# Twenty-four extra transposes inside a recurrence, twelve on float32 cells and twelve on float32r cells

## The reference

```
z = sigmoid(x @ Wz + bz);  h_tilde = x @ Wh + bh
a, b = 1 - z, z * h_tilde
h[s] = a[s] * h[s-1] + b[s]          (a scan along the sequence)
x = layernorm(x + sigmoid(h @ Wg + bg) * h)
```

## Time and profile before

| | |
|---|---|
| median of three runs | 854.05 us |
| the profiled execution, whole time | 854.72 us |
| its span, first to last instruction | 852.9 us |
| busy share of the span: TensorE / VectorE / ScalarE / GpSimd | 94 / 77 / 71 / 50 % |
| TensorE busy from 33 to 45.4 us (two steps of the recurrence) | 12.40 of 12.40 us |
| mean granted TensorE clock | 0.996 |

### The profile page before, as it was taken

One profiled execution on the slowest core, in us unless ns is written; L12 is line 12 of the kernel. 1 busy time (PEld: TensorE's weight loads), 2 busy tenths in 40 slices (PEclk: granted clock), 3 DMA queues, 4 the chain that ended last, 5 costly groups with the idle time before them and its releaser, 6 DMA issues.

```text
span 852.9 us, 20803 instructions
## 1 busy us (share of the span) xinstructions
PE 805.5 (94%) x6837; PEld 605.5 (71%) x6837; DVE 654.1 (77%) x2466; ACT 609.7 (71%) x1595; POOL 427.7 (50%) x459
## 2 busy tenths in 40 slices
PE   9998999999999988999999999999999999999996
PEld 8876776766667766677777767667766777677785
DVE  4987778888998766777777667673888888985667
ACT  4547887888784367877877777774899999985341
POOL 2255667666644155254552534224665666425763
PEclk9999999999999999999999999999999999999999
DMA  9401761112103368977868688756122211100001
GB/s 321 157 25 45 224 194 51 55 60 81 70 15 124 124 216 269 295 218 242 277 205 268 215 247 255 239 177 212 42 66 67 66 66 66 64 2 1 26 25 50
DMA packets 105392, 115.64 MB, mean 136 GB/s; under 512 B 28589, under 2 KB 93869, under 8 KB 105030
## 3 DMA queue, kind: packets, MB, share of 16 engines
q1 hardware_dynamic: 104724, 113.97, 41.8%
q10 hardware_dynamic: 562, 0.35, 0.1%
HBM read 48.70 MB, written 51.82 MB: 118 GB/s over the span
## 4 chain that ended last, share of the span: by engine, by line
PE 46%; ACT 9%; DVE 5%; issue 3%; DMA 2%; POOL 1%; SPq 0%; DVEq 0%; ACTq 0%; POOLq 0%
PE bank L1544 7%; PE bank L242 6%; PE bank L250 4%; PE bank L2259 4%; PE bank L1559 3%; PE bank L2245 3%; ACT bias_area L2597 2%; PE bank L2276 2%; PE bank L1528 2%; PE bank L1585 2%; PE bank L1595 2%; PE bank L2309 2%; PE bank L2353 2%; PE bank L2347 2%; ACT Sx L1750 2%
## 5 line engine op out<-in xcount | busy, mean ns | idle before, releaser
L242 PE MATMUL bank<-x_feat,w_all_mats 128*128 128x256 f32 x384 | 92.7, 386 | 1.8 <-ACT q_full L358 0.6
L2994 POOL TENSOR_TENSOR bnd<-bnd,consts 128x60 f32<-128x60 f32 x64 | 18.1, 305 | 142.0 <-DMA bnd<-band_scratch 142.0
L242 PEld LDWEIGHTS bank<-x_feat,w_all_mats 128*128 128x128 f32 x384 | 70.5, 191 | 14.3 <-ACT rw L2639 3.8
L2597 ACT ACTIVATE bias_area<-bias_area,mq_two 128x256 f32<-128x256 f32 x128 | 66.2, 529 | 0.0
L1003 DVE COPY q_heads<-bank 128x512 f32<-128x512 f32 x64 | 42.0, 684 | 24.4 <-PE bank L717 24.4
L2773 DVE COPY q_heads<-bank 128x512 f32<-128x512 f32 x64 | 41.2, 683 | 23.2 <-PE bank L2259 23.2
L896 ACT ACTIVATE Sx<-Sx,mq 128x256 f32<-128x256 f32 x128 | 54.4, 498 | 5.4 <-DVE mq L995 5.4
L1750 ACT ACTIVATE Sx<-Sx,mq 128x256 f32<-128x256 f32 x128 | 54.3, 500 | 3.4 <-DVE mq L1848 3.4
L904 ACT ACTIVATE q_heads<-bank 128x512 f32<-128x512 f32 x64 | 37.8, 590 | 26.3 <-PE bank L717 26.3
L1856 DVE COPY q_heads<-bank 128x512 f32<-128x512 f32 x64 | 42.0, 684 | 17.0 <-PE bank L1544 17.0
L896 ACT ACTIVATE Pr<-Pr,mq 128x256 f32<-128x256 f32 x128 | 54.4, 502 | 0.9 <-DVE mq L995 0.9
(11 more groups left out here) (309 smaller groups left out, 2384.8 us busy)
## 6 DMA issues: line engine op xcount, KB each, us to landing
dist<-skew_scratch SPq DMA_DIRECT2D x64, 296.0 KB, 4.1
skew_scratch<-rw SPq DMA_DIRECT2D x30, 588.0 KB, 4.5
bnd<-band_scratch SPq DMA_DIRECT2D x64, 108.0 KB, 2.6
band_scratch<-bias_area SPq DMA_DIRECT2D x32, 162.0 KB, 2.5
band_scratch<-bias_area SPq DMA_DIRECT2D x32, 148.0 KB, 2.1
skew_scratch<-dist SPq DMA_DIRECT2D x4, 1024.0 KB, 7.1
context_values<-dist SPq DMA_DIRECT2D x8, 512.0 KB, 2.6
v_two<-context_values SPq DMA_DIRECT2D x8, 512.0 KB, 4.3
```

The source lines that it names most:

```text
L242: last = pe.matmul(dst[:, m * S:(m + 1) * S], w[:, k, m * P:(m + 1) * P], rhs[:, k, :], start=(k == 0), stop=(k == FT - 1))
L2597: last = act.activation(rows_of(n, g)[:, t, :], rows_of(n, g)[:, t, :], ACT.Exp, bias=mq_two[:, n % 2, g, t:t + 1], scale=-1.0, accum_out= ...
```

## The change

- SyncE: at the end of `first_loads` it waits for the small tables and all thirteen matrices, and then issues two copies of 64 KB within SBUF: the identity `ident` and one 128x128 block of `sa_Wq`, into two float32r tensors within the space of `q_par` (which the attention fills later).
- TensorE: after `gate_product(4)` it waits for these copies, and turns the block of `sa_Wq` twelve times from float32 into bank 3 and twelve times from the float32r copy into bank 5. All twelve of a kind have the same input; four places of a bank are written three times each.
- VectorE: after its loop, with `norm` of batch 5 begun, it waits for the last transpose, copies 16 columns of bank 3 to SBUF, subtracts them from 16 columns of bank 5, and adds the result times 1e30 to the 16 ones of `v_two` for one tile of tokens. Each of the three waits for the one before.

```diff
+        raw_ident = exact_cells("raw_ident", [P, P], q_par_at)
+        raw_x = exact_cells("raw_x", [P, P], q_par_at + 4 * P)
+        raw_in, raw_mm, raw_steps = sem("raw_in"), sem("raw_mm"), sem("raw_steps")
+        raw_rows = sb("raw_rows", [P, 2, H])
+        def raw_loads(sp):
+            sp.wait_ge(loaded_small, 48)
+            sp.wait_ge(loaded_w, 16 * len(WMATS[3:]))
+            sp.dma_start(raw_ident[:, :].bitcast(F32), ident[:, :]).then_inc(raw_in, 16)
+            sp.dma_start(raw_x[:, :].bitcast(F32), W["sa_Wq"][:, 0, 0:P]).then_inc(raw_in, 16)
+        def raw_turns(pe):
+            pe.wait_ge(raw_in, 32)
+            for i in range(12):
+                pe.transpose(bank[3][:, i % 4 * P:(i % 4 + 1) * P], W["sa_Wq"][:, 0, 0:P], ident[:, :])
+            for i in range(12):
+                last = pe.transpose(bank[5][:, i % 4 * P:(i % 4 + 1) * P].bitcast(F32R), raw_x[:, :], raw_ident[:, :])
+            last.then_inc(raw_mm, 1)
+        def raw_differences(dve):
+            dve.wait_ge(raw_mm, 1)
+            dve.tensor_copy(raw_rows[:, 0, :], bank[3][:, 0:H]).then_inc(raw_steps, 1)
+            dve.wait_ge(raw_steps, 1)
+            dve.tensor_tensor(raw_rows[:, 1, :], bank[5][:, 0:H], raw_rows[:, 0, :], ALU.subtract).then_inc(raw_steps, 1)
+            dve.wait_ge(raw_steps, 2)
+            ones_col = v_two[:, 0, 0, :, DH]
+            dve.scalar_tensor_tensor(out=ones_col, in0=raw_rows[:, 1, :], scalar=1e30, in1=ones_col,
+                                     op0=ALU.mult, op1=ALU.add)
...
                 gate_product(pe, b)
+                if b == 4:
+                    raw_turns(pe)
...
                 gru_norm_begin(dve, b - 1)
+            raw_differences(dve)
...
             sp.dma_start(consts[:, :], consts_d).then_inc(rel_in, 16)
+            raw_loads(sp)
```

## The result

The changed kernel took 857.03 us (median of 18 runs, 855.42 to 860.9), the kernel before 854.12 (18 runs). The ratio is 1.0038, with a 95% interval of 1.0028 to 1.0048: 3.2 us slower (2.4 to 4.1). The forecast was 856.5 us in 855.3 to 858.1, slower.

What follows compares the result with a forecast made beforehand. TensorE, without idle time in the recurrence, was taken as the bound. Its 1.32 + 0.78 = 2.1 us and VectorE's 0.4 make 2.5, added to 854.05: 856.55, say 856.5 us, range 855.3 to 858.1.

Steps and rivals of the forecast that it cites:

- TensorE is full in the recurrence, and what is put there reaches both engines: Two recurrence steps: TensorE busy 12.40 of 12.40 us, VectorE 11.49; work added between 37.65 and 39.48 delays both.
- Twelve float32 transposes, 1.32 us: TensorE after `gate_product(4)`: twelve at 0.11 us each, priced from four such transposes in the recurrence.
- Twelve float32r transposes, 0.78 us: TensorE, behind the float32 ones: twelve at 0.065 us each, between bounds of 0.06 and 0.11 to 0.119.
- the shorter load hides under a pass of 0.06: Float32r transposes on TensorE: the 141 ns weight load was assumed hidden by the pass, giving 0.065 us each.
- Nothing for the products behind: TensorE products after the added transposes: they come 2.1 us later, with no extra time of their own in the sum.
- VectorE, 0.55 us, of which 0.4 on the path: Three operations ahead of `gated_input(7)`: 0.16 us vanishes waiting for GpSimd, 0.4 reaches `gate_product(7)`; ends 0 and 0.8.
- a sign of being wrong: The forecast is wrong if TensorE's wait before `gate_product(7)` does not grow with VectorE's 0.4 us.
- SyncE's wait and copies, nothing: SyncE's loads: copies land more than 5 us before TensorE asks at 39.5; delayed loads behind them cost nothing.
- The sum, 2.5: Whole kernel: TensorE's 2.1 us plus VectorE's 0.4, added to 854.05 us.
- Nothing takes the delay up: Attention: no independent work found to absorb the delay; the rival, absorbed by idle time, gave 854.0 us, chance 0.08.
- The clock: Rival: clock halves behind the transposes, 3.5 us of products take 7, in all 6 us slower, 860; chance 0.05.
- the rival with equal prices: Float32r transposes cost what float32 ones do: 24 x 0.11 = 2.64 plus 0.4, 857.1 us; chance 0.25.

Runs made afterwards that it cites:

- the price list: Against the changed kernel: six lots of 24 transposes or products in place of the 24 transposes, VectorE's three operations left out; one execution, 870.45 us.
- the repetition: The changed kernel, unchanged, timed again against the kernel before: 858.05 us against 854.55, ratio 1.0044 (1.0028 to 1.0060).
- gap version: Changed kernel with its 24 transposes moved to the attention's first round, where TensorE waits 0.97 us, without VectorE's operations: 856.06 us, ratio 1.0021 to the kernel before.
- 96 and 96: Changed kernel with 96 float32 and 96 float32r transposes instead of 12 and 12: 874.63 us against 854.36 for the kernel before, ratio 1.0245.

## Why the prediction was right

- *TensorE is full in the recurrence, and what is put there reaches both engines.* Right: no idle time before the first transpose, and VectorE's wait grew by 2.35.
- *Twelve float32 transposes, 1.32 us.* Measured 1.23 in the changed kernel; over 96 of them 0.108 each, so 1.30. The row of four transposes in the same stage priced them well. (The last one of a lot is overlapped by the float32r one behind it.)
- *Twelve float32r transposes, 0.78 us.* Too low: 1.05, or 0.0875 each. The step that failed is the sentence that the shorter load hides under a pass of 0.06. In the price list the pitch follows the columns to load, 0.0875 for 128 and 0.060 for 64, at the same pass. The value lies between the two that I had bounded it by, 0.06 and 0.11, and near the middle; I had taken the end of the bfloat16 row, whose loads are reported with a median of 98 ns, against 141 here. With the load's row set against the load's row the middle would have been the better choice.
- *Nothing for the products behind.* 0.08 us was missing.
- *VectorE, 0.55 us, of which 0.4 on the path.* 0.53 and 0.28. The size was right; of it 0.23 vanished between `gated_input(7)` and xn, where VectorE had waited for GpSimd, not 0.16 (53.01 - 51.99 = 1.02 us before, and 0.79 now). The path failed. The prediction let the rest reach TensorE at `gate_product(7)`, and named as a sign of being wrong that the wait there does not grow. It did not: 0.34 us in the kernel before, in the changed one and without VectorE's operations. TensorE met the delay at `turn_xn(5)`, where its wait grew by 0.28, and carried it from there.
- *SyncE's wait and copies, nothing.* Right, alone and in the whole.
- *The sum, 2.5.* In the length 2.68: 0.27 too little for float32r, 0.08 for the product behind, 0.12 too much for VectorE and 0.09 for float32, and 0.04 that these roundings leave. That the sum lies within 0.2 of the traces is in part luck: 0.35 too little and 0.21 too much nearly cancel.
- *Nothing takes the delay up.* Right for the attention: the offset to the kernel before is 2.79 to 2.82 from 60 to 284 us, and 192 transposes pass through as whole as 24. Behind 842 us 0.35 of it is gone.
- *The clock.* It did not fall behind the transposes, and not behind eight times as many; it did in the price list. The rival's price was too high by its own rows: a mean of 0.66 over five us is 3.4 us at half the clock, which loses at most 1.7 us, not 3.5. The fall at the block boundary cost 1.26.

The timed difference, 3.2 us (2.4 to 4.1) and in the repetition 3.8 (2.4 to 5.1), lies above the 2.68 of the traces, though both intervals contain it. The median of 857.03 is nearer to the rival with equal prices (857.1) than to the forecast (856.5); the times can't part the two, the traces do, and they refute that rival. All four timed comparisons lie above their lengths: the gap version's is 1.8 (0.5 to 3.0) against 0.6, and that of 96 and 96 is 20.9 (19.1 to 22.7), whose lower end is just above the 19.08 of its length. The profiled execution was the fastest of the 18 of the changed kernel, and the 0.35 us lost behind 842 us make the excess greater. What the traces don't show of it stays open.

## What to carry to other kernels

Price an instruction by its place first: 24 transposes cost 2.4 us where their engine had no idle time, and where it was waiting for another engine their delay had vanished 15 us later (with 0.6 us in the length from later stages). For short TensorE instructions set the load against the pass, and take the price from a row with the same load. Before you divide a lot's time by its count, read the granted clock of that very stretch: one lot of the price list ran at half of it and looked like a puzzle. To see an effect of 0.3% in a kernel that spreads by more, compare two rows of each trace that bracket the change: the stage between them repeated within 0.1 us.

## What the runs showed of the hardware

- A float32r transpose of 128x128 costs 0.087 us, a float32 one 0.108; with 64 columns to load the float32r one costs 0.060. Taken in turn, a pair costs 0.17 instead of 0.195.
- A float32r product with 128 or 64 moving columns costs 0.11 us, as much as one with 256 in this kernel. With 64 columns to load it took 0.107 at a granted clock of 0.50.
- In one trace the granted clock stayed at 1.00 through 18.7 us of transposes alone. In the price list it fell to 0.50 from 51.14 to 54.55 us, behind 11 us in which TensorE had no idle time.
- In eight of thirteen traces the first float32 products start every 0.43 us instead of 0.22, until the trace's record of the clock begins, 6.0 to 10.7 us after the start; windows over that time show 1.00 all the same.
- Behind one block boundary, with TensorE idle for 1.1 us, the same program found the clock full in one execution and fallen in another, which is worth some 1.2 us; it was full in five of thirteen traces. Another 1.9 us, seen in two of thirteen, comes from the first products, which there run at half their rate until 9.6 and 10.7 us.
